# Order of the first pair and width of the last pair in a two-stage cross-attention kernel

## The reference, cut to what matters

```
q, k, v = x @ w_q.T, c @ w_k.T, c @ w_v.T
x1      = x + alpha * softmax(q @ k.T / sqrt(512)) @ v @ w_o.T
g       = g_w @ c + g_b            # 128 x 512, conv over the 256 rows
theta   = theta_w @ x1 + theta_b   # 128 x 512
phi     = phi_w @ c + phi_b        # 128 x 512
y       = ((theta.T @ phi) / 512) @ g.T
out     = batchnorm(w_w @ y.T + w_b) + x1
```

## Time and profile before

| what | value |
|---|---|
| median of 3 runs | 404.56 us (404.21 to 405.39) |
| the profiled execution, its own time | 403.8 us |
| its span, first to last instruction | 402.0 us |
| mean granted TensorE clock | 0.989 |
| PE busy | 386.7 us, 96% of the span |
| DVE busy | 291.6 us, 73% |
| ACT busy | 187.6 us, 47% |
| bytes moved by DMA | 68.13 MB, 169 GB/s over the span |

### The profile page before, as it was taken

The page is one execution under the profiler, slowest core; times in us unless marked ns, Lnnn a source line. Parts: engine busy times, 40 slices in busy tenths (PEclk is TensorE's granted clock), DMA queues, the critical chain, the costliest instruction groups (busy, mean ns, idle before and its releaser), DMA issues.

```text
span 402.0 us, 5804 instructions
## 1 busy us (share of the span) xinstructions
PE 386.7 (96%) x1967; PEld 329.9 (82%) x1967; DVE 291.6 (73%) x567; ACT 187.6 (47%) x385; POOL 1.8 (0%) x7
## 2 busy tenths in 40 slices
PE   8999893999999999999999999999999999999994
PEld 5888782888988898889888898889888898889873
DVE  4998545588569955887679864996678864996684
ACT  3476443562375425562465426551475336551350
POOL 1000000000000000000000000000000000000000
PEclk9999997899999999999999999999999999999999
DMA  7993640355655464536655464636555454025512
GB/s 252 364 368 120 238 137 20 141 174 185 201 178 176 151 222 144 210 103 231 173 170 178 151 219 130 235 97 233 166 170 181 170 190 123 26 78 163 155 49 104
DMA packets 55803, 68.13 MB, mean 169 GB/s; under 512 B 4592, under 2 KB 46320, under 8 KB 52720
## 3 DMA queue, kind: packets, MB, share of 16 engines
q1 hardware_dynamic: 55792, 67.99, 51.1%
HBM read 49.09 MB, written 18.87 MB: 169 GB/s over the span
## 4 chain that ended last, share of the span: by engine, by line
PE 93%; DVE 3%; ACT 1%; DMA 1%; issue 0%; DVEq 0%; SPq 0%; ACTq 0%
PE bank L318 23%; PE bank L319 23%; PE bank L320 23%; PE bank L377 6%; PE bank L347 5%; PE bank L365 4%; PE bank L366 4%; PE bank L367 4%; DMA cT_raw<-w_q 1%; DVE c_sides L700 1%; DVE xb L883 0%; DVE xb L857 0%; DVE tT_lo L700 0%; DVE x_lo L700 0%; ACT x_hi L519 0%
## 5 line engine op out<-in xcount | busy, mean ns | idle before, releaser
L318 PE MATMUL bank<-ov_hi,c_sides 128*128 128x512 f32 x128 | 50.0, 391 | 0.0
L319 PE MATMUL bank<-ov_lo,c_sides 128*128 128x512 f32 x128 | 50.0, 390 | 0.0
L319 PE MATMUL bank<-c_sides,qk_hi 128*128 128x512 f32 x128 | 50.0, 390 | 0.0
L320 PE MATMUL bank<-c_sides,qk_lo 128*128 128x512 f32 x128 | 49.9, 390 | 0.0
L318 PE MATMUL bank<-c_sides,qk_hi 128*128 128x512 f32 x128 | 49.8, 389 | 0.0
L320 PE MATMUL bank<-ov_hi,c_sides 128*128 128x512 f32 x128 | 49.8, 389 | 0.0
L595 ACT ACTIVATE probs<-bank,neg_max 128x256 f32<-128x256 f32 x32 | 14.9, 471 | 56.9 <-DVE neg_max L803 56.9
L365 PE MATMUL bank<-tT_hi,xT_hi 128*128 128x256 f32 x128 | 36.3, 283 | 1.4 <-DVE tT_lo L700 1.4
L700 DVE TENSOR_TENSOR vo_lo<-bank,vo_hi 128x512 fp32r<-128x512 f32 x32 | 21.5, 687 | 21.0 <-ACT vo_hi L519 20.9
L366 PE MATMUL bank<-tT_lo,xT_hi 128*128 128x256 f32 x128 | 36.2, 283 | 0.0
L367 PE MATMUL bank<-tT_hi,xT_lo 128*128 128x256 f32 x128 | 36.2, 283 | 0.0
(11 more groups left out here) (129 smaller groups left out, 866.4 us busy)
## 6 DMA issues: line engine op xcount, KB each, us to landing
cT_raw<-ctx_t SPq DMA_DIRECT2D x8, 1024.0 KB, 4.8
xT_raw<-x_t SPq DMA_DIRECT2D x8, 1024.0 KB, 4.9
c_raw<-ctx_n SPq DMA_DIRECT2D x8, 1024.0 KB, 4.9
xb<-x SPq DMA_DIRECT2D x16, 512.0 KB, 3.9
out<-xb SPq DMA_DIRECT2D x15, 512.0 KB, 2.7
gram_moved<-gram_blocks SPq DMA_DIRECT2D x16, 256.0 KB, 2.3
gram_blocks<-gram_moved SPq DMA_DIRECT2D x64, 64.0 KB, 2.0
moved<-blocks SPq DMA_DIRECT2D x16, 256.0 KB, 2.4
```

Of the source, the lines that this page charges most:

```text
L318: pe.matmul(dst, ahi, bhi, start=(k == 0), stop=False)
L319: pe.matmul(dst, ahi, blo, start=False, stop=False)
L320: mm = pe.matmul(dst, alo, bhi, start=False, stop=(k == k_tiles - 1))
```

## The change

In front of the first pair's scores PE now does `w_g_bias`, which stood behind them. In the first pair T1 moves behind both deltas and writes banks 6 and 7 instead of 4 and 5; the wait for `t1_made` moves from in front of delta(1) to in front of both_rows(1). ACT and DVE do u ahead of cT, x1_rows ahead of t1_rows, x1_part ahead of t1_part; ACT's `c_sums` moves behind theta_part(0). On SP the wait for `c_summed` and the load behind it move past the load of the transposed context and the Gram sends and fetches. In the last pair theta, output and the stores of batch 1 are done in two column halves of 256 (three stores of 256, 128 and 128 KB in place of two of 256 KB), in other banks.

```diff
 WG_BANK, WG_BIAS_BANK = 4, 5
+FIRST_T1_BANK = [6, 7]
+LAST_THETA_BANK = [5, 0]
+LAST_OUT_BANK = [[4, 7], [2, 3]]
...
-    def store_tile(p, b, ct):
-        sp.dma_start(out[p, :, b, ct], xb[:, b, ct]).then_inc(tile_stored, 16)
-
...
     def pair(p, first=False, prefetch=True, last=False):
-        two, four = counts(sp, p, 2, [1, 2, 3, 4]), counts(sp, p, 4, [2, 3, 4, 8])
+        two, four = counts(sp, p, 2, [1, 2, 3, 4]), counts(sp, p, 4, [2, 4, 5, 6, 8])
         turned = counts(sp, p, 16, [16, 32])
...
         if prefetch:
-            sp.wait_ge(c_summed, four[8])
-            load_c(p + 2)
+            if not first:
+                sp.wait_ge(c_summed, four[8])
+                load_c(p + 2)
             sp.wait_ge(cT_lo, two[4])
...
         if prefetch:
+            if first:
+                sp.wait_ge(c_summed, four[8])
+                load_c(p + 2)
             sp.wait_ge(xT_lo, two[4])
...
         if last:
+            sp.wait_ge(out_made, four[4])
+            sp.dma_start(out[p, :, 1, :, 0:L], xb[:, 1, :, 0:L]).then_inc(tile_stored, 16)
             for ct in range(KL):
-                sp.wait_ge(out_made, four[3 + ct])
-                store_tile(p, 1, ct)
+                sp.wait_ge(out_made, four[5 + ct])
+                sp.dma_start(out[p, :, 1, ct, L:H], xb[:, 1, ct, L:H]).then_inc(tile_stored, 16)
         else:
...
     sp.wait_ge(stored[1], 16 * (PAIRS - 1))
-    sp.wait_ge(tile_stored, 16 * KL)
+    sp.wait_ge(tile_stored, 16 * (1 + KL))
...
-    def w_g_phi(b):
-        product(bank[T1_BANK[b]][:, 0:L], lambda k: cut(u, every, 2 * b + k, every),
+    def w_g_phi(b, banks=T1_BANK):
+        product(bank[banks[b]][:, 0:L], lambda k: cut(u, every, 2 * b + k, every),
                 lambda k: cut(wg, every, k, every), KS).then_inc(t1_done, 1)
...
+
+    def last_theta(half):
+        at = slice(half * L, (half + 1) * L)
+        product(bank[LAST_THETA_BANK[half]][:, 0:L], lambda k: cut(theta_w, every, k, every),
+                lambda k: cut(x1, every, 1, k, at), KL).then_inc(theta_done, 1)
+
+    def last_output(half, ct):
+        at = slice(half * L, (half + 1) * L)
+        product(bank[LAST_OUT_BANK[half][ct]][:, 0:L], lambda k: cut(t1, every, 1, tile(ct)),
+                lambda k: cut(theta, every, 1, at), 1).then_inc(out_done, 1)
...
     t_tile(3)
+    pe.wait_ge(ww_scaled, 1)
+    pe.wait_ge(g_bias_made, 1)
+    pe.wait_ge(tT_lo, 2)
+    w_g_bias()
...
         if first:
-            pe.wait_ge(ww_scaled, 1)
-            pe.wait_ge(g_bias_made, 1)
-            w_g_bias()
             pe.wait_ge(small_lo, 2)
...
             values(1, st)
-        if first:
-            pe.wait_ge(wg_lo, 1)
-            pe.wait_ge(wg_bias_made, 1)
-            pe.wait_ge(u_lo, 1)
-            w_g_phi(0)
-            w_g_phi(1)
         pe.wait_ge(vo_lo, four[2])
...
             delta(0, lt)
-        pe.wait_ge(t1_made, two[2])
+        if first:
+            pe.wait_ge(wg_lo, 1)
+            pe.wait_ge(wg_bias_made, 1)
+        else:
+            pe.wait_ge(t1_made, two[2])
         pe.wait_ge(vo_lo, four[4])
...
             pe.wait_ge(x1_lo, four[4])
-            theta_rows(1)
+            for half in range(2):
+                last_theta(half)
             pe.wait_ge(t1_lo, two[1])
...
             pe.wait_ge(t1_lo, two[2])
-            pe.wait_ge(theta_lo, two[2])
-            for ct in range(KL):
-                output(1, ct)
+            for half in range(2):
+                pe.wait_ge(theta_lo, two[2 + half])
+                for ct in range(KL):
+                    last_output(half, ct)
             return
+        if first:
+            pe.wait_ge(u_lo, 1)
+            w_g_phi(0, FIRST_T1_BANK)
+            w_g_phi(1, FIRST_T1_BANK)
         pe.wait_ge(cT_lo, two[4])
         both_rows(0)
+        if first:
+            pe.wait_ge(t1_made, 2)
         both_rows(1)
...
         landed = counts(act, p, 16 * BLOCKS, [16 * BLOCKS])
-        two, four = counts(act, p, 2, [-1, 0, 1, 2]), counts(act, p, 4, range(-2, 9))
+        two, four = counts(act, p, 2, [-1, 0, 1, 2, 3]), counts(act, p, 4, range(-2, 9))
...
         vo_part(1, 1)
+        if first:
+            u_part()
         if not last:
...
             cT_parts(loads[32])
-        if first:
-            u_part()
+        for lt in range(KL):
+            x1_part(0, lt)
+        if first:
             t1_part(0)
             t1_part(1)
-            c_sums(loads[32])
-        for lt in range(KL):
-            x1_part(0, lt)
         if not last:
...
             theta_part(0)
-            theta_part(1)
+            for half in range(2):
+                at = slice(half * L, (half + 1) * L)
+                act.wait_ge(theta_done, two[2 + half])
+                hi(theta[0][:, 1, at], bank[LAST_THETA_BANK[half]][:, 0:L], theta_hi,
+                   bias=col[:, THETA_B:THETA_B + 1])
             return
...
         theta_part(0)
+        if first:
+            c_sums(loads[32])
         xT_part(0, loads[32])
...
-        def t1_rows(b):
+        def t1_rows(b, banks=T1_BANK):
             dve.wait_ge(t1_done, two[b + 1])
...
             dve.scalar_tensor_tensor(out=t1_raw[:, b], in0=wg_bias[:], scalar=v[:, b:b + 1],
-                                     in1=bank[T1_BANK[b]][:, 0:L], op0=ALU.mult,
+                                     in1=bank[banks[b]][:, 0:L], op0=ALU.mult,
                                      op1=ALU.add).then_inc(t1_made, 1)
...
         vo_part(1, 1)
+        if first:
+            u_rows()
+            u_part()
         if not last:
             cT_parts([two[3], two[4]])
-        if first:
-            u_rows()
-            u_part()
+        x1_rows(0)
+        if first:
             dve.wait_ge(wg_bias_made, 1)
-            t1_rows(0)
-            t1_rows(1)
+            t1_rows(0, FIRST_T1_BANK)
+            t1_rows(1, FIRST_T1_BANK)
+        for lt in range(KL):
+            x1_part(0, lt)
+        if first:
             t1_part(0)
             t1_part(1)
-        x1_rows(0)
-        for lt in range(KL):
-            x1_part(0, lt)
         if not last:
...
             theta_part(0)
-            theta_part(1)
-            for b in range(2):
+            for half in range(2):
+                at = slice(half * L, (half + 1) * L)
+                dve.wait_ge(theta_hi, two[2 + half])
+                dve.scalar_tensor_tensor(out=theta[1][:, 1, at], in0=bank[LAST_THETA_BANK[half]][:, 0:L],
+                                         scalar=col[:, THETA_B:THETA_B + 1],
+                                         in1=theta[0][:, 1, at].bitcast(F32), op0=ALU.add,
+                                         op1=ALU.subtract).then_inc(theta_lo, 1)
+            for ct in range(KL):
+                out_rows(0, ct)
+            for half in range(2):
+                at = slice(half * L, (half + 1) * L)
                 for ct in range(KL):
-                    out_rows(b, ct)
+                    dve.wait_ge(out_done, four[2 + 2 * half + ct + 1])
+                    dve.scalar_tensor_tensor(out=xb[:, 1, ct, at], in0=bank[LAST_OUT_BANK[half][ct]][:, 0:L],
+                                             scalar=out_bias[:, ct:ct + 1], in1=xb[:, 1, ct, at],
+                                             op0=ALU.add, op1=ALU.add).then_inc(out_made, 1)
             return
```

More of the change, by code:

```diff
@@ L911, in pair @@
                 vo_part(1, 1)
-                if not last:
-                    cT_parts([two[3], two[4]])
                 if first:
@@ L916, in pair @@
                     u_part()
+                if not last:
+                    cT_parts([two[3], two[4]])
+                x1_rows(0)
+                if first:
                     dve.wait_ge(wg_bias_made, 1)
-                    t1_rows(0)
-                    t1_rows(1)
+                    t1_rows(0, FIRST_T1_BANK)
[3 more added lines that the diff above has]
+                if first:
                     t1_part(0)
                     t1_part(1)
-                x1_rows(0)
-                for lt in range(KL):
-                    x1_part(0, lt)
                 if not last:
```

## The result

| | before | after |
|---|---|---|
| median (range), runs | 405.02 us (404.21 to 406.30), 6 | 395.07 us (394.64 to 395.53), 6 |
| ratio, 95% interval | | 0.9753 [0.9735, 0.9770] |
| profiled execution, its span | 403.8, 402.0 | 395.53, 393.7 |
| mean granted clock of the span | 0.989 | 0.997 |

The forecast was 395.1, range 394.1 to 397.4. It was worked out from a median of 404.56 for the kernel before (three runs); over six runs that median is 405.02. The medians differ by 9.95 us, the two profiled executions by 8.27.

A forecast was written before the change was run, and what follows sets the result against it. PE was taken to bound the kernel, busy or last in the chain for 93% of the span. First pair 9.2 plus last pair 0.3 made 9.5 us, so 404.56 would become 395.1, range 394.1 to 397.4.

The forecast's parts named there:

- The first pair: First pair on PE: both_rows begins 9.41 us earlier, minus 0.18 for a new wait, making 9.2 us gained.
- w_g_bias in the wait for tT_lo: First pair, PE: w_g_bias fits into the 1.41 us wait before the scores, so everything behind them comes 1.11 us earlier.
- rival C: First pair: fetched squares land late, so u_lo's wait moves behind the deltas; up to 2.4 us, 397.5; chance 0.05.
- The wait for t1_made: First pair, PE in front of both_rows(1): DVE ends t1_rows at 69.91, so PE loses 0.18 us.
- The slow clock: First pair, T1 and deltas on PE: they took 8.50 us against 6.90 at unit prices, so 1.6 us gained.
- A loop pair of other than 44.6 us: Pairs after the first: listed sign of something the prediction had not thought of; no change was forecast there.
- Both cost nothing: SP, first pair: sending cT's load at about 68 and loading pair 2's context later was put at no cost.
- I take nothing for it: First pair, ACT and DVE lag: tT_lo(3) at 89.26 for scores at 89.39, so 0 taken; ends 0 and 2.1 us.
- Rival B: ACT and DVE lag: c_sums and postponed cT make PE wait before pair 1's scores; 1 to 2.1 us; chance 0.18.
- The theta halves: Last pair: halved theta ends the second theta_lo 0.46 us earlier, so batch 0's store issues at 396.42 instead of 396.88.
- the split store: Last pair, batch 1: 1 KB rows at 356 GB/s instead of 394, so 512 KB take 1.47, not 1.33; 0.14 us lost.
- the end moves with the first store: Last pair: DMA engines are full from first store to last byte, so the end gains 0.46 us, not DVE's 0.2.

The follow-up runs named there:

- experiment 5: The kernel before with only w_g_bias moved in front of the first pair's scores; median 403.40 us, ratio 0.9959.
- Experiment 6: The changed kernel with ACT and DVE of the first pair doing cT ahead of u again; median 395.71 us, ratio 0.9770.
- experiment 11: The kernel before with 24 matmuls on zeros in front of the first pair's wait for u_lo; median 403.20 us, ratio 0.9956.
- experiment 3: The kernel before with only the last pair's part of the change; median 404.42 us, ratio 0.9981, profiled execution 405.07 us.
- experiment 8: The changed kernel with batch 0's load of x behind the probabilities' sends and fetches in all pairs but the first; median 394.27 us, ratio 0.9729.
- experiment 9: The changed kernel with the first pair's c_sums behind batch 0's cross_copy instead of behind theta_part(0); median 394.62 us, ratio 0.9748.
- experiment 10: The changed kernel with c_sums in ACT's gap, the x load behind the probabilities, and the last pair's batch 0 stored as two tiles; median 394.01 us, ratio 0.9733.
- experiment 7: The changed kernel with batch 1 of the last pair stored as two whole tiles in rows of 2 KB; median 394.97 us, ratio 0.9747.
- experiment 2: The changed kernel with the last pair's theta, output and stores as they were before; median 395.63 us, ratio 0.9761.
- experiment 4: The changed kernel with batch 0 of the last pair stored as two tiles of 256 KB; median 394.91 us, ratio 0.9747.

## Why the prediction was right, and where it was not

**The first pair (forecast 9.2, measured 9.31)** went step by step as reckoned. w_g_bias in the wait for tT_lo: 1.11 forecast, 1.31 by the start of T1 in experiment 5, 1.4 by its medians. u_lo "65.2", measured 65.31. The fetch that no row showed landed at 62.54 (forecast 62.5), so rival C, u still late, fell. Deltas to T1: no gap. T1 1.44, measured 1.43. The wait for t1_made, 0.18 forecast, cost 0.35 with the restart. S0 to S1 comes to 46.58 by the text's times (89.39 - 42.81) and was 46.50. Experiment 6 shows that u ahead of cT, a part of the edit to which I gave no price of its own, carries 1.0 of this.

**The slow clock (forecast 1.6)** was right for the profiled execution, and experiment 11 confirms it: 55.81 - 54.21 = 1.60. What I did not see is that it is not a constant. In experiment 3 it cost 2.7, and the runs of before scatter over 2 us where those of the changed kernel scatter over 0.9. Could it be dearer on average than in before's profile, so that 9.95 came off the median and only 8.27 off the profiled execution? Experiment 5, with 1.4 by medians and 0.61 in the pair profiled, points that way. The record speaks against a large part of it: of the 36 runs of before in the three groups only four have a mean granted clock of 0.986 or 0.987, as the dear case of experiment 3 has, and these took 405.7 to 406.3; before's profile has 0.989, which is usual. Experiment 11, which takes the slow clock away, gains 1.7 by medians. A plainer part of the gap is that before's profile has the earliest S0 of the thirteen, 0.46 under the middle one, and that after's has the longest wait at delta(1). No run separates these. The Trainium skill (TensorE: Matmul & The Clock Gate, The HAM clock gate) has the clock set by how busy TensorE has been recently; the 0.50 at 69 us behind the wait and the 1.00 of experiment 11 agree.

**The pairs between (forecast 0, measured +1.42; +0.82 when run again)** is where a step failed. "A loop pair of other than 44.6 us" was on my list as something that I had not thought of, and the second pair took 46.05. The step is the one on SP: "Both cost nothing", and on DVE's and ACT's lag "I take nothing for it". I had carried the lag forward to the last tT_lo, found it in time by 0.1 us, and stopped at S1. It was in time: 89.27 for 89.65. But the same lag delays phi's squares, the text even has their send at 90 without asking what goes out behind it. The load of x does, and it crowds the send of batch 0's probabilities. Experiments 8 and 9 take away the one and the other link, and the second pair is back at 44.6 in both; experiment 10, with both, has 44.7. The link from the load to the landing is shown in two profiles without the load (2.3 us) and seven with it close ahead (4.3 to 5.3); the link from c_sums to the wait rests on one. Rival B named the right cause, the lag with c_sums in it, but the wrong place; at S1 PE waits for nothing. By medians, the repairs are worth 0.4 (394.27 against 394.71, different chips) and 0.1 (394.62), less than the 0.8 to 1.4 of the traces; their intervals overlap that of the changed kernel, so the wait's mean cost stays open.

**The last pair (forecast 0.3, measured 0.70 to 0.75).** The theta halves were priced at 0.46 and gave 0.45 (experiment 7 against 2); the first store moved from X + 4.51 to X + 4.08. The mis-sized term is the split store. It was put at 0.14 us lost, since rows of 1 KB would run at 356 GB/s and rows of 2 KB at 394. But the whole 512 KB pass as fast in 1 KB rows (1.66 us) as in 2 KB rows (1.68 in experiment 7, 1.70 in before), and neither comes near the 1.47 and 1.33 that I had. Single packets of 1 KB do cost more per byte in the middle of the stream (median 46 ns against 84 to 86 for 2 KB, 8%); over all packets it is 3% (mean 47 against 91), as some of the 2 KB packets take long. The Trainium skill (DMA: Bandwidth & Descriptors, Why small descriptors are slow), from which I had estimated under 5%, lies between the two. And "the end moves with the first store" left out what lies behind the last byte: it fell from 1.25 us to 1.0. So instead of -0.14 the split store is worth +0.24.

**The sum.** From the profiled execution: +0.34 in front of S0, -9.31, +1.42, -0.75 make -8.30 for spans of 402.0 and 393.7. Against the forecast of 9.5 the profiles fell 1.2 short. The forecast of 395.1 was met to 0.03 us all the same, because misses cancel: the second pair lost 0.5 to 1.4 us in the six executions of kernels that have the changed first pair and no repair, the last pair gained 0.4 more than forecast, and the median of before from which I subtracted was 0.46 below the one measured with more runs. Taken from 405.02, a gain of 9.5 would have given 395.5. The forecast was right on the mechanism of nine tenths of the gain, and lucky in the last half us.

## What to carry to other kernels

When a bound engine gets faster, follow the engines that now lag to the end of the next stage, and on every queue, not just to the next join: here the lag was harmless at the scores and cost PE up to 1.1 us some 22 us later, through a load that slid in front of a small urgent send. The long wait of TensorE cost more than its length here, by 1.6 us in one execution and 2.7 in another, so read more than one profile before pricing such a wait; where it couldn't be filled with work, idle matmuls recovered that part. At the end of a kernel look at what lies behind the last byte, beside the time of the first: smaller last stores shortened it here. And a DMA that is late only matters beyond the time at which the queue would be free for the next one.

## What the runs showed of the hardware that I had not expected

- The same code gets its clock back at different times behind the same idle stretch of 6.55 us: by 72.5 us in one execution, beyond 75 in another. Price 1.6 and 2.7 us.
- A 256 KB send issued within 1.5 us of a 512 KB load on the same queue landed in 4.3 us, once in 5.3; with no load ahead it landed in 2.3. In the worst case the stretches show the tail of few engines, not a full system:

```profile
98.50:99.00 0.50, 0.50 (x4) 0.42 (x3) 0.50 (x3) 0.07 (x1) 0.00 (x0) 1.00 0.22 68
99.00:99.50 0.50, 0.50 (x3) 0.39 (x3) 0.50 (x3) 0.50 (x2) 0.00 (x0) 1.00 0.06 25
```

  A share of 0.06 is one engine of 16 (1/16 = 0.0625), which still has bytes of a transfer when the others are done. Among the packets of the load one of 4 KB runs from 97.14 to 98.74, 1.6 us where the median is 0.16. What held it isn't shown.
- The last 1 MB, by packets: 512 KB pass in 1.46 us in rows of 4 KB (after), in 1.68 to 1.75 in rows of 2 KB (experiments 7 and 4), in 1.66 in rows of 1 KB (after). The step from 4 to 2 KB cost more than that from 2 to 1.
- The time from the last byte to the end of the span is 1.0 us where the last store is of 128 KB in rows of 1 KB (eight profiles), and 1.25 to 1.3 where it is of 256 KB in rows of 2 KB (five profiles).
- SP's issue of a DMA, 0.37 us as a rule, took 1.0 to 1.3 us in six profiles (second pair), and was through 0.3 to 0.4 behind the end of a 16 KB transfer on the queue that the page calls "instruction".
